# Gathering the rows of 42 edge tiles early, parking them in DRAM as blocks, and loading them back with plain transfers

## The reference

```python
q = (x @ Wq + bq).reshape(n, H, C)          # H = 8 heads of C = 32
k = (x @ Wk + bk).reshape(n, H, C)
v = (x @ Wv + bv).reshape(n, H, C)
e = (edge_attr @ We).reshape(-1, H, C)
kj = k[src] + e
alpha = jnp.einsum('ehc,ehc->eh', q[dst], kj) / jnp.sqrt(jnp.float32(C))
amax = jax.ops.segment_max(alpha, dst, num_segments=n)
ea = jnp.exp(alpha - amax[dst])
denom = jax.ops.segment_sum(ea, dst, num_segments=n)
alpha = ea / (denom[dst] + 1e-16)
msg = (v[src] + e) * alpha[:, :, None]
out = jax.ops.segment_sum(msg, dst, num_segments=n)
out = out.reshape(n, H * C) + (x @ Ws + bs)
x = _layernorm(x + out, axis=-1, eps=1e-05)
```

## Time and profile before

| | us |
|---|---|
| median of 3 runs | 1547.55 (1539.19 to 1552.91) |
| the profiled execution, its own time | 1557.84 |
| its span in the profile | 1556.1 |
| PE busy | 1371.3 (88%) |
| DVE busy | 1036.4 (67%) |
| POOL busy | 811.8 (52%) |
| ACT busy | 761.1 (49%) |
| the 392 gathers on POOL (L518) | 409.1, 1044 ns each |
| the 196 scatters on POOL (L533) | 209.3, 1068 ns each |

### The profile page before, as it was taken

The page is one execution under the profiler, slowest core; times in us unless marked ns, Lnnn a source line. Parts: engine busy times, 40 slices in busy tenths (PEclk is TensorE's granted clock), DMA queues, the critical chain, the costliest instruction groups (busy, mean ns, idle before and its releaser), DMA issues.

```text
span 1556.1 us, 27452 instructions
## 1 busy us (share of the span) xinstructions
PE 1371.3 (88%) x8027; PEld 1197.2 (77%) x8027; DVE 1036.4 (67%) x3142; ACT 761.1 (49%) x2168; POOL 811.8 (52%) x749
## 2 busy tenths in 40 slices
PE   7699999999999998888898888887988797888893
PEld 5588888888888887777777777776877686767782
DVE  4688877777777785665556566665665665656684
ACT  3454555555555554544444444454554344444462
POOL 1544444344344446565656565655656465656545
PEclk9899999999999999897988897988988798989897
DMA  5887767666676642232323233333323232323211
GB/s 189 259 272 261 231 219 235 223 225 219 215 236 222 221 154 86 74 84 81 94 80 89 86 99 84 101 94 89 107 94 97 75 113 89 100 89 102 89 44 42
DMA packets 95660, 216.62 MB, mean 139 GB/s; under 512 B 29653, under 2 KB 33433, under 8 KB 95512
## 3 DMA queue, kind: packets, MB, share of 16 engines
q1 hardware_dynamic: 67096, 145.52, 28.2%
q0 software_dynamic: 28416, 69.35, 15.2%
HBM read 145.06 MB, written 77.79 MB: 143 GB/s over the span
## 4 chain that ended last, share of the span: by engine, by line
PE 69%; another core or an unknown queue 13%; issue 8%; DVE 5%; ACT 3%; DMA 1%; POOL 1%; DVEq 0%; SPq 0%; POOLq 0%; ACTq 0%
PE bank L1136 35%; PE bank L1116 21%; PE bank L1128 5%; PE bank L1149 2%; PE bank L1148 2%; PE bank L1145 1%; PE bank L1166 1%; DVE sd L846 1%; ACT area L670 1%; ACT mv_part L651 1%; DVE alpha L878 0%; PE bank L1172 0%; PE bank L1178 0%; DMA area<-bq_dram 0%
## 5 line engine op out<-in xcount | busy, mean ns | idle before, releaser
L518 POOL DMA_INDIRECT rows_in<-xrows_dram,slot x392 | 409.1, 1044 | 129.5 <-issue 101.0
L1116 PE MATMUL bank<-w_y,xT 128*128 128x256 f32 x1568 | 372.5, 384 | 24.2 <-DVEq L801 10.7
L1136 PE MATMUL bank<-w_kv,sd 128*128 128x512 f32 x1176 | 351.0, 433 | 13.8 <-issue 12.5
L1116 PEld LDWEIGHTS bank<-w_y,xT 128*128 128x128 f32 x1568 | 288.5, 192 | 58.9 <-DVE y L811 11.1
L1136 PEld LDWEIGHTS bank<-w_kv,sd 128*128 128x128 f32 x1176 | 231.8, 207 | 66.3 <-issue 27.1
L509 POOL TENSOR_TENSOR rstd<-var,half 128x4 f32<-128x4 f32 x98 | 119.6, 1220 | 284.7 <-DVE var L819 283.1
L603 ACT ACTIVATE square<-y 128x256 f32<-128x256 f32 x392 | 159.8, 409 | 182.0 <-DVE var L819 123.0
L533 POOL DMA_INDIRECT out_dram<-area,where x196 | 209.3, 1068 | 71.4 <-issue 58.4
L1136 PE MATMUL bank<-w_s,sd 128*128 128x256 f32 x1176 | 211.9, 315 | 22.5 <-issue 22.1
L1136 PE MATMUL bank<-w_q,sd 128*128 128x264 f32 x1176 | 199.9, 307 | 0.3 <-issue 0.3
L1136 PEld LDWEIGHTS bank<-w_e,e_part 128*128 128x128 f32 x1176 | 177.6, 200 | 28.1 <-issue 9.5
(11 more groups left out here) (126 smaller groups left out, 1856.0 us busy)
## 6 DMA issues: line engine op xcount, KB each, us to landing
xT<-xt_dram SPq DMA_DIRECT2D x98, 512.0 KB
out_dram<-y SPq DMA_DIRECT2D x98, 512.0 KB
eT<-et_dram SPq DMA_DIRECT2D x98, 256.0 KB
dst_all<-dst_row_dram SPq DMA_DIRECT2D x49, 256.0 KB
rows_in<-xrows_dram,slot POOLq DMA_INDIRECT x392
out_dram<-area,where POOLq DMA_INDIRECT x196
bounds<-area SPq DMA_DIRECT2D x74, 4.0 KB
area<-flag_rows_dram SPq DMA_DIRECT2D x28, 28.0 KB
```

The costliest lines, as they stand in the source:

```text
L518: nc.gpsimd.indirect_dma_start(out=rows_in[:, t % RIN, i, :], out_offset=None, in_=xrows, in_offset=bass.IndirectOffsetOnAxis(ap=slot[:, t ...
L1116: ins = nc.tensor.matmul(node_bank(p)[:, i * D:(i + 1) * D], xT[:, u % RX, c, 2 * b + i, :], w_y[:, c, :], start=(c == 0), stop=(c == KC - 1))
L1136: ins = nc.tensor.matmul(to, rows[a][:, c * P:(c + 1) * P], weights[b][:, c, :], start=(first and n == 0), stop=(last and n == len(terms) ...
```

## The change

Tiles 50, 53, 56 and so on up to 173 (42 of them, every third) get their rows in another way. In slot n (n = 0 to 41), beside the node pairs, POOL gathers the two times 128 rows of the n-th of these tiles into one of two extra places of SBUF (`staged`), SP stores them in the next slot to a DRAM block `ahead[n]` (256 KB), and four slots before the tile is turned SP loads the block back into the tile's place of `rows_in` with two plain DMAs of 128 KB. For these tiles the gather in the edge part is gone. The ring `rows_in` has four places in the place of six, and the two places given up are the two of `staged`, so SBUF use is unchanged. PE's turn waits for `gathered` or for `reloaded`, by the kind of tile.

```diff
@@
-RIN = 6
+RIN = 4
@@
+AHEAD, AHEAD_FROM, AHEAD_STEP = 42, 50, 3
@@
+    ahead = nc.dram_tensor("ahead", [AHEAD, P, 2 * D], F32)
@@
-        rows_in = sb("rows_in", [P, RIN, 2, D])
+        rows_in = sb("rows_in", [P, RIN + 2, 2, D])
+        staged = rows_in[:, RIN:]
@@
+        def ahead_of(t):
+
+            n, left_over = divmod(t - AHEAD_FROM, AHEAD_STEP)
+            return n if left_over == 0 and 0 <= n < AHEAD else None
+
+        def arrivals(t):
+
+            return sum((ahead_of(u) is None) == (ahead_of(t) is None) for u in range(t % RIN, t + 1, RIN))
+
@@ sync
+            def store_staged(n):
+                if 0 <= n < AHEAD:
+                    sp.wait_ge(staged_in[n % 2], (n // 2 + 1) * 32)
+                    sp.dma_start(ahead.ap()[n], staged[:, n % 2].rearrange("p i d -> p (i d)")).then_inc(staged_out[n % 2], 16)
+
+            def load_rows(t):
+                n = ahead_of(t)
+                if n is not None:
+                    sp.wait_ge(turned, t - RIN + 1)
+                    sp.wait_ge(staged_out[n % 2], (n // 2 + 1) * 16)
+                    for i in range(2):
+                        sp.dma_start(rows_in[:, t % RIN, i, :],
+                                     ahead.ap()[n, :, i * D:(i + 1) * D]).then_inc(reloaded[t % RIN], 16)
 
             def edge_slot(s):
@@
                     if p is not None:
                         node_pair(p)
+                store_staged(s - 1)
+                load_rows(s + RIN)
@@ gpsimd
             def gather(t):
-                if not is_tile(t):
+                if not is_tile(t) or ahead_of(t) is not None:
                     return
@@
+            def gather_ahead(n):
+                if not 0 <= n < AHEAD:
+                    return
+                t = AHEAD_FROM + n * AHEAD_STEP
+                over(pool, staged_out[n % 2], n // 2 * 16)
+                if n == 0:
+                    pool.wait_ge(slots_in[1], 16)
+                for i in range(2):
+                    nc.gpsimd.indirect_dma_start(
+                        out=staged[:, n % 2, i, :], out_offset=None, in_=xrows,
+                        in_offset=bass.IndirectOffsetOnAxis(ap=slot[:, t // EG, t % EG, i:i + 1], axis=0),
+                    ).then_inc(staged_in[n % 2], 16)
@@
                     if p is not None:
                         node_pair(p)
+                    if k == 0:
+                        gather_ahead(s)
@@ tensor
             def turn(t):
-                pe.wait_ge(gathered[t % RIN], (t // RIN + 1) * 32)
+                pe.wait_ge((gathered if ahead_of(t) is None else reloaded)[t % RIN], arrivals(t) * 32)
```

More of the change, by code:

```diff
@@ L218, in build @@
         gathered = [sem(f"gathered{r}") for r in range(RIN)]
+        reloaded = [sem(f"reloaded{r}") for r in range(RIN)]
+        staged_in = [sem(f"staged_in{p}") for p in range(2)]
+        staged_out = [sem(f"staged_out{p}") for p in range(2)]
         turned = sem("turned")
```

## The result

The changed kernel takes **1455.02 us** (median of 4 runs, 1449.28 to 1457.79); the kernel before takes 1543.37 us beside it (1534.69 to 1552.91). The ratio is 0.9396, 95% interval 0.9354 to 0.9437: 88 us less, against the 1465 us forecast and well inside its range. The profiled execution took 1455.97 us (span 1454.2), 102 us less than the profiled one of before.

The account below looks back on a forecast made before the run. Beside the node pairs PE bounds; with edges alone 7.0 us of each 25.4 us group are lost, going with POOL's indirect DMAs. Profiled 1557.8 us minus 91 plus 5 is 1472; median 10 lower: 1463, rounded to 1465; range 1375 to 1558.

Parts of the forecast that it names:

- What bounds: Node part bound by PE; with edges alone, 7.0 us of each 25.4 us group lost above PE's 18.4.
- The gathers that leave, 91 us: Edges-alone part: 84 gathers leave, 2.71 fewer indirect DMAs a group over 31 groups, 91 us less.
- the slope: Edges-alone groups: 1.09 us for each indirect DMA, from 19.4 us at 7.5 of them to 25.4 at 13.
- the window at 1472.06: Group at the end of the edge part, counted as 4 gathers and 3 scatters, taking 19.7 us.
- That alone is off the path, since POOL idles now.: Edge part: POOL's own time falls from 18.4 us a group to 13 to 16, by itself gaining nothing.
- late completions: Edge part: PE's results reach other engines 5 us late, seen as "remote" waits of DVE 110.5 and ACT 106.4 us.
- The gathers that come in, 5 us: Beside the node pairs: 84 gathers added, two a slot in slots 0 to 41; cost 5 us, bounds 0 and 20.
- the slower rival: Loss goes with POOL's share of time and moves to the node part: +182 us there, 1644 us; chance 0.13.
- The ring of four, 0: Edge gathers needed three slots later instead of five: no cost unless POOL slips by over 7 us.
- The last groups at 25 us as before: Sign of being right: the last five groups, tiles from 174, still take 25 us.
- Nothing gained: Edge-part loss stays, or follows each DMA wherever issued at 0.54 us: 1535 to 1563 us; chance 0.15.
- The loss vanishes: Edge-part loss needs POOL at work as long as PE, so 217 us go: 1336, range 1330 to 1400; chance 0.14.

Follow-up runs that it names:

- ring of four only: The changed kernel without parking: all 196 tiles gathered in their own slots, ring of four places; 1343.03 us, ratio 1.0041 to the kernel before.
- 66 tiles: The changed kernel with 66 tiles parked in place of 42, three in two slots, same two places; 1448.47 us, ratio 0.9367 to the kernel before.
- three operations a tile: Changed kernel with all 146 tiles from 50 on loaded plain (wrong rows), plus three POOL powers of 128x4 per tile; 1432.53 us, ratio 0.9468.
- 146 tiles plain: Changed kernel with SP loading all 146 tiles from 50 on from contiguous (wrong) rows, no gathers there; 1308.35 us, on another chip 1309.74.

## Why the prediction was right, and where it was not

**What bounds.** Right for the node part: PE is full at 1.00 before and after. For the edge part the runs found two things above PE's own 18.4 us, and the prediction saw one. Over a stretch of groups each takes PE's 18.4 us or POOL's own time, whichever is longer. On some chips it takes longer than both, and the more so the more indirect DMAs POOL has in it. Of the 7.0 us lost in a group of before, 3.2 are PE busy for longer at the lower granted clock (757.04 / 35 = 21.6 us for what takes 18.4) and 3.8 are PE idle; the prediction speaks of the clock and did not split the loss.

| indirect DMAs in a group | POOL's work, us | group, chips with before at 1337 and 1338 | group, chips with before at 1514 to 1545 |
|---|---|---|---|
| 13 | 19.6 us | 19.62 | 25.45 |
| 11 | 16.9 | 18.57 | 21.83, 22.85 |
| 9 | 14.3 | 18.13 | 19.91, 20.10, 21.07 |
| 5 | 8.2 to 8.9 | 18.43 | 18.50 |
| 5 and 12 operations | 22.2 | | 22.24 |

(19.62 is of ring of four only; several values stand for several runs.)

**The gathers that leave, 91 us.** The size held, 3.17 us a group against 2.95, 98 us against 91, and so did what carries it: with fewer gathers late the waits for "remote" shrink. One count in the slope is wrong. It took the window at 1472.06 as 4 gathers and 3 scatters; POOL's timeline has four scatters in it (1476.33, 1480.74, 1482.25, 1487.32). With 8 DMAs for the mean of the two windows the slope is 6.0 / 5 = 1.20 us and the gain 2.71 x 1.20 x 31 = 101 us. The order held too (9 DMAs shorter than 11 in every trace). One slope for all counts was too even. From 13 to 11 it is (25.45 - 22.85) / 2 = 1.30, from 11 to 9 0.89, from 9 to 5 0.40 where 20.10 and 18.50 stand on one chip. Why it falls was not separated.

**"That alone is off the path, since POOL idles now."** For the pair above nothing contradicts this: no engine waits for POOL in the edge part of either trace. As a statement on the kernel it failed, and with it the expectation of a like gain elsewhere. The step took 0.97 us for a gather from one line of the earlier trace rows, where the 280 gathers average 1.057 us and the scatters 1.069; and 8 x 1.27 + 5 x 1.31 + 1.5 is 18.2, not 18.4. With the means, 8 x 1.36 + 5 x 1.37 + 1.5 is 19.2 us, and measured 19.6, over PE's 18.4 and not equal to it. On the chips without late completions that excess is the whole gain: 31 x 1.19 = 37 us less 5 for the ring, 31 us measured. How much of the 98 us of the pair comes from POOL's shorter work is open. If the floor and the lateness added up it would be 37; by the waits of the trace it would be nothing.

**The gathers that come in, 5 us.** It was 0. The window of slots 0 to 6 reached a DMA share of 0.90 (0.96 was worked out) with PE full, and the rest 0.80 as forecast. POOL's wait for `var` gave room as said; the 0.59 share of POOL cost nothing there, so the slower rival falls. The `staged_out` wait that the prediction named as the danger, from 3 us up, reached 4.4 us and cost nothing at one tile a slot; with 66 tiles it reached 8.3 us and broke the run.

**The ring of four, 0.** Right in the changed kernel. With 13 DMAs a group, on a chip without late completions, it costs 4.7 us; PE's turn waits there up to 3.1 us for a gather, and that this is the cause is not shown. At the start it gave back 3 us, which I had not seen.

**The last groups at 25 us as before:** 24.69 and 23.91.

**The rivals.** *Nothing gained*: refuted, since gathers that move are not paid again. A rule stood behind that rival: the Trainium skill, "DMA: Bandwidth & Descriptors", section "Issuing engines are not separate DMA queues", says that issuing from several engines saves only the sequencer's time to initiate a DMA, "usually small relative to the DMA itself". On the two quiet chips the traces agree that POOL's time is what is saved, and not that it is small: about 1.1 us and 0.30 us per indirect DMA, which for 13 of them and one `root` came to 19.6 us, more than all of PE's work in a group. *The loss vanishes* had the right end and condition there (1305 us, groups of 18.4, POOL at work at least as long as PE), but not its price: 31 us were gained and not 217. The forecast of 1465 rested on a chip with late completions, as the profile of before showed one, and held because the pair was timed on such a chip; on the two quiet ones the change is worth 31 us, a third of the 88.

**Open.** What makes a completion late on one chip and not on another. POOL's being busy does not bring it about by itself (three operations a tile), nor does DMA traffic as such (share 0.42 with 146 tiles plain and few waits for "remote", 0.31 and many of them before). It goes with indirect DMAs at 9 and more in a group. Beside the node pairs 16 of them in 46 us have no such wait, and 20 in 50 us one, of 2.3 us; 14 in 27 us, as the node pairs end, have it. Whether gathers and scatters count alike in it, and whether a plain load issued by POOL would bring it, was not run on such a chip.

## What to carry to other kernels

Add up an engine's own time over one period of the loop from the mean durations and the gaps, DMA issues included, and compare it with the bound's; an engine that idles in the profile may still be the next floor, here at 19.6 us under groups of 25.4. Work that can be issued in a stretch where the issuing engine has room cost nothing here until one wait behind it lasted longer than that room: the third tile in two slots gained 1.7 us in each of some 20 groups and lost 4.6 us in every four slots beside the node pairs, and more at their start. And hold a profile against a second chip before pricing a loss that no instruction explains.

## What the runs showed of the hardware

- The same kernel took 1338, 1514 and 1545 us on different chips; with 5 indirect DMAs a group in its edge part it took 1308 and 1310. The traces of the slower chips have "remote" waits (337 us in all on ACT, DVE and POOL, 582 to 1260 us, in the kernel before) that go with POOL's indirect DMAs, and a lower granted clock beside them; the eight traces of the faster chips, with 5 to 13 indirect DMAs a group, have none.
- An indirect DMA of 128 rows of 1 KB takes POOL 1.04 to 1.22 us (means of the runs) and 0.30 us before the next; a plain one of the same size 0.565 us. POOL's 128x4 power took 1.15 and 1.18 us (means of the two runs that added it) and follows the last without a gap.
- TensorE's granted clock went with PE's waiting: in the edge part 0.88 with 13 indirect DMAs a group on a slower chip, 0.95 to 0.99 with fewer or with POOL as the bound, 1.00 wherever PE was full, on every chip. On one chip and with the same work on PE it was 1.00 with 146 tiles plain and 0.96 with three POOL operations a tile, where PE was busy 584 of 668 us.
